# Moving the two layer normalisations of the dense stage from VectorE to ScalarE, with shift and scale worked out on GpSimd

## The reference, cut to what matters

```
out = res + _lin(out, Wf, bf)                          # out: the first attention's result, res: its input
on  = _ln(out, g2, b2)                                 # layer norm with gain and bias
ffn = _lin(relu(_lin(on, Wr1, br1)), Wr2, br2)         # 128 -> 256 -> 128
x   = x + (out + ffn)                                  # called x1 in the kernel
x   = x + _L0_ffn_ref(_layernorm(x), W1, b1, W2, b2)   # 128 -> 512 -> 128, no activation between
```

## Time and profile before

| | us |
|---|---|
| median of 3 runs | 1803.19 |
| lowest and highest run | 1800.59, 1816.49 |
| the profiled execution | 1800.75 |
| its span | 1799.0 |
| the dense stage in it | 822 to 1038 |

### The profile page before, as it was taken

The page is one execution under the profiler, slowest core; times in us unless marked ns, Lnnn a source line. Parts: engine busy times, 40 slices in busy tenths (PEclk is TensorE's granted clock), DMA queues, the critical chain, the costliest instruction groups (busy, mean ns, idle before and its releaser), DMA issues. The chain is left out here.

```text
span 1799.0 us, 45960 instructions
## 1 busy us (share of the span) xinstructions
PE 1516.6 (84%) x13604; PEld 1309.6 (73%) x13668; DVE 1456.8 (81%) x3554; ACT 767.1 (43%) x1731; POOL 866.8 (48%) x1116
## 2 busy tenths in 40 slices
PE   5999999999999999993767648888888888888887
PEld 3999988889889988982655426666666666666665
DVE  5589999999999999974888756778787877777874
ACT  1566656666656665651222213333333333333331
POOL 4356656666666665544565443333333333333331
PEclk8999999999999999996888968999999999999986
DMA  4433222222332222213333133333333333333330
GB/s 137 136 109 90 81 77 79 80 80 86 87 87 87 79 81 77 79 31 94 100 103 87 50 82 93 95 95 95 94 99 93 96 94 96 95 96 97 92 88 17
DMA packets 181693, 158.10 MB, mean 88 GB/s; under 512 B 12529, under 2 KB 163185, under 8 KB 181618
## 3 DMA queue, kind: packets, MB, share of 16 engines
q1 hardware_dynamic: 181618, 157.17, 30.2%
HBM read 113.09 MB, written 44.04 MB: 87 GB/s over the span
## 5 line engine op out<-in xcount | busy, mean ns | idle before, releaser
L587 PE MATMUL a_bank<-a_vp,a_prob 128*128 128x96 f32 x4096 | 635.2, 261 | 0.0
L587 PEld LDWEIGHTS a_bank<-a_vp,a_prob 128*128 128x128 f32 x4096 | 610.6, 192 | 5.6
L481 ACT ACTIVATE a_prob<-a_bank 128x512 f32<-128x512 f32 x512 | 305.9, 598 | 268.2 <-PE a_bank L571 267.3
L675 DVE TENSOR_REDUCE a_nmax<-a_bank 128x2 f32<-128x512 f32 x512 | 345.7, 681 | 49.2 <-PE a_bank L556 41.9
L556 PE MATMUL a_bank<-a_k_st,a_q_st 96*128 96x256 bf16 x1024 | 260.6, 278 | 38.4 <-DVE a_nmax L675 35.4
L571 PE MATMUL a_bank<-a_q_st,a_k_st 120*128 120x256 bf16 x1024 | 281.7, 276 | 3.2 <-POOL a_q_st L344 3.2
L1607 PE MATMUL c_o_bank<-c_vb,c_prob 128*128 128x96 f32 x1024 | 179.4, 301 | 30.1 <-DVE c_ad L1890 29.2
L1765 DVE TENSOR_REDUCE c_nmax<-c_bank 128x4 f32<-128x512 f32 x256 | 166.0, 683 | 38.7 <-PE c_bank L1577 37.1
L344 POOL TENSOR_SCALAR a_q_st<-a_mt 24x2048 bf16<-24x2048 bf16 x64 | 121.4, 1896 | 138.6 <-PE a_bank L571 94.3
L1481 ACT ACTIVATE c_prob<-c_bank 128x256 f32<-128x256 f32 x256 | 98.8, 386 | 186.4 <-PE c_bank L1557 184.8
L1607 PEld LDWEIGHTS c_o_bank<-c_vb,c_prob 128*128 128x128 f32 x1024 | 144.1, 203 | 41.4 <-DVE c_ad L1890 29.1
(11 more groups left out here) (200 smaller groups left out, 3072.4 us busy)
## 6 DMA issues: line engine op xcount, KB each, us to landing
a_q_st<-scratch_a_parts_dram SPq DMA_DIRECT2D x64, 288.0 KB
a_k_st<-scratch_a_parts_dram SPq DMA_DIRECT2D x192, 96.0 KB
c_q_st<-scratch_c_parts_dram SPq DMA_DIRECT2D x64, 288.0 KB
c_k_st<-scratch_c_parts_dram SPq DMA_DIRECT2D x192, 96.0 KB
scratch_a_parts_dram<-a_parts SPq DMA_DIRECT2D x32, 384.0 KB, 2.7
scratch_c_parts_dram<-c_parts SPq DMA_DIRECT2D x32, 384.0 KB, 2.7
a_x<-in_x SPq DMA_DIRECT2D x32, 128.0 KB, 3.2
scratch_y<-a_y SPq DMA_DIRECT2D x32, 128.0 KB, 2.9
```

The costliest lines, as they stand in the source:

```text
L481: act.activation(prob[h % 4][:, :, :].rearrange("p a b -> p (a b)"), t_ps[h % 2][:, :], ACT.Exp).then_inc(exped, 1)
L587: mm = pe.matmul(o_ps[g % 2][:, at:at + VC], prob[h % 4][:, c, t * P:(t + 1) * P], vp[o][:, c, :], start=c == 0, stop=c == NT - 1)
L675: dve.tensor_reduce(nmax[:, t, 2 * g:2 * g + 2], s_ps[t][:, :].rearrange("p (h k) -> p h k", h=2), AX.X, ALU.max, negate=True).then_inc(ma ...
```

## The change

`normed` goes from VectorE's queue to ScalarE's. There it is an activation with the function Identity, `z = rs * r + shift`, with two operands that differ by partition (token). `shift` is `-mean * rs`, which GpSimd's `norm` now works out with two more operations on 128 x 4 numbers, `negm` and `shift`, so that its semaphore counts four steps a unit (NORM = 4). The first normalisation stands between `ao_t` and `on`; the second stands between `on` and the two hidden activations. VectorE gets two waits for the buffers that ScalarE now reads (`x1` and `r`, both two deep), and its waits before the moments are for GpSimd's use of `mv`.

```diff
+        negm, shift = two("negm", [P, C]), two("shift", [P, C])
...
-        N_LOAD, N_LATE = 4, 3
+        N_LOAD, N_LATE, NORM = 4, 3, 4
...
                 pool.tensor_scalar(var[k][:, :], mv[k][:, :, 1], EPS, 1.0, ALU.add, ALU.mult).then_inc(norm_d[k], 1)
-                pool.wait_ge(norm_d[k], 2 * n + 1)
+                pool.tensor_scalar(negm[k][:, :], mv[k][:, :, 0], -1.0, 1.0, ALU.mult, ALU.mult
+                                   ).then_inc(norm_d[k], 1)
+                pool.wait_ge(norm_d[k], NORM * n + 2)
                 pool.tensor_tensor(rs[k][:, :], var[k][:, :], half[:, :], ALU.pow).then_inc(norm_d[k], 1)
+                pool.wait_ge(norm_d[k], NORM * n + 3)
+                pool.tensor_tensor(shift[k][:, :], negm[k][:, :], rs[k][:, :], ALU.mult).then_inc(norm_d[k], 1)
...
+            def normed(k, n, src, dst):
+                act.wait_ge(norm_d[k], NORM * (n + 1))
+                for c in range(C):
+                    act.activation(dst[:, c, :], src[:, c, :], ACT.Identity, scale=rs[k][:, c:c + 1],
+                                   bias=shift[k][:, c:c + 1]).then_inc(z_d[k], 1)
+
...
                 if has(j, u, 1):
+                    if later(j, n, 3):
+                        act.wait_ge(zt_p, n - 2)
+                    normed(0, n - 1, r[1 - i], z[1 - i])
                     act.wait_ge(zt_p, n)
...
+                if has(j, u, 2):
+                    if later(j, n, 4):
+                        act.wait_ge(z1t_p, n - 3)
+                    normed(1, n - 2, x1[i], z1[i])
+                if has(j, u, 1):
                     if later(j, n, 3):
                         act.wait_ge(f_p, n - 2)
...
-            def normed(k, n, src, dst):
-                dve.wait_ge(norm_d[k], 2 * (n + 1))
-                for c in range(C):
-                    dve.tensor_scalar(dst[:, c, :], src[:, c, :], mv[k][:, c, 0:1], rs[k][:, c:c + 1],
-                                      ALU.subtract, ALU.mult).then_inc(z_d[k], 1)
...
                     if later(j, n, 4):
                         dve.wait_ge(xb_d, n - 3)
+                        dve.wait_ge(z_d[1], (n - 3) * C)
...
                     if later(j, n, 3):
-                        dve.wait_ge(z_d[1], (n - 2) * C)
+                        dve.wait_ge(norm_d[1], NORM * (n - 2))
...
                     if later(j, n, 2):
                         dve.wait_ge(xr_d, 2 * (n - 1))
+                        dve.wait_ge(z_d[0], (n - 1) * C)
...
                     if later(j, n, 1):
-                        dve.wait_ge(z_d[0], n * C)
-                if has(j, u, 2):
-                    if later(j, n, 4):
-                        dve.wait_ge(z1t_p, n - 3)
-                    normed(1, n - 2, x1[i], z1[i])
-                if has(j, u, 0):
+                        dve.wait_ge(norm_d[0], NORM * n)
                     moments(0, n, r[i])
```

## The result

| | before | with the change |
|---|---|---|
| median, us | 1809.66 (4 runs, 1800.59 to 1816.49) | 1732.41 (4 runs, 1731.13 to 1735.42) |
| profiled execution | 1800.75 | 1733.57 |
| first stage, to the first load of `dense` | 822.72 | 821.11 |
| dense stage | 215.92 | 175.27 |
| `attention_b`, to the end of the span | 760.36 | 735.42 |

The change took 0.959 of the time before, with a 95% interval of 0.9538 to 0.9641. The forecast was 1763 us with a range of 1752 to 1775, so the sign was right and the time lies 20 us outside the range. The span fell by 67.2 us: 40.65 in the dense stage (forecast 37.7), 24.9 in `attention_b`, whose code is unchanged, and 1.6 in the first stage. The first stage's end lay between 821.4 and 823.1 in all other kernels of this study, none of which alters that stage, so the 1.6 us is mostly spread.

The account below looks back on a forecast made before the run. VectorE's own queue was taken to set the dense stage's 12.21 us step. Twelve steps at 9.6 us save 31.3, plus 3.2 and 3.5, less 0.3: 37.7 us off 1800.75 gives 1763 us, range 1752 to 1775.

Parts of the forecast that it names:

- Removed from VectorE: Dense stage: eight instructions per unit, 5.93 us, and 1.85 us of waits leave VectorE, which no longer bounds anything.
- ScalarE's activation: Added normalisation in the dense stage: 0.49 us per 128x128 activation, 1.66 us per block of four.
- The least and the longest bound: ScalarE's block of four activations: 1.29 us if the second operand is free, 1.96 us without overlap.
- the rival at 1813: GpSimd holds ScalarE's activations as it does VectorE's, 1.26 us each, slower than before; chance 0.02.
- the one at 1811: Rival: ScalarE is the slower engine for normalisation, each block 0.32 us longer, 10 us in all; chance 0.01.
- GpSimd's block: GpSimd's numbers for one normalisation, with negm and shift added: 1.8 us instead of 1.30, bounds 1.7 and 2.1.
- loop A: Dense stage, through GpSimd and ScalarE's second normalisation, hidden activations, second MLP matmul and x1: 9.2 us a unit.
- H: Dense stage loop between second MLP matmuls, through TensorE and ScalarE's first normalisation: 9.2 us a unit.
- TensorE's clock: Granted clock of 0.93 in the dense stage lengthens the loop by 3.8%, 9.55 us; 9.6 taken as the step.
- Filling and draining: Dense stage's ends: 0.3 us lost in filling, 3.2 gained from unit 2 to 3, 3.5 gained at the end.
- the four rivals about the step: Dense steps: 10.4 us (1773, chance 0.13), 8.6 (1750, 0.09), 11.3 or more (1785 up, 0.04), held activations (1813, 0.02).

Follow-up runs that it names:

- e4: The changed kernel with only the first normalisation on ScalarE, the second back on VectorE between r and its moments; 1756.24 us, 0.9714.
- e5: The changed kernel with ScalarE's first normalisation ahead of the copy to ao_t; 1736.26 us, 0.9605.
- e3: The changed kernel with ScalarE's second normalisation behind the two hidden activations, not ahead of them; 1768.79 us, 0.9782.
- e6: The changed kernel with ScalarE's second normalisation behind the hidden activations and TensorE's transpose of z1 behind the second MLP matmul; 1735.72 us, 0.9602.
- e7: The changed kernel with the new orders of e5 and e6 together; 1731.1 us, 0.9568.
- e13: The kernel before with a small GpSimd write in attention_b that puts its last subtraction 0.28 us later; 1735.63 us, 0.9621.
- e12: The changed kernel run once more, unaltered; 1731.16 us, 0.9548.

## Why the prediction was wrong, and where it was right

**What failed** is the first sentence of its reading, "since only the dense stage changes": `attention_b` was carried over at 760 us. It took 735, and in no term of the sum, no rival and no bound was there room for that. I had read a window of that stage for its granted clock, but not asked whether its time is the same whenever it is entered. The spread of the runs shown, 16 us for one and the same program, was a hint that it is not. Of the 29.5 us by which the span's fall exceeded the sum, 24.9 are this stage, 1.6 the first stage, 3.0 the dense stage.

**Removed from VectorE:** as predicted; it is busy 72 us of the dense stage and waits for TensorE.

**ScalarE's activation** was put at 0.49 us and a block at 1.66; measured 482 to 485 ns and 1.65. The least and the longest bound (1.29, 1.96) weren't needed. No activation was held by GpSimd (all 128 took 477 to 496 ns), so the rival at 1813 is out. So is the one at 1811: for this shape VectorE is quicker only where GpSimd rests, and e4 shows the block back at 2.92 us beside it.

**GpSimd's block** was put at 1.8 us plus 0.1 for the hand-over; `var` to ScalarE's block is 1.94. Its work per unit is 8.1 us, not 8.6; GpSimd never fills its step, but through loop A its second block sets the time of most units.

**Loops H and A** were put at 9.2 us each. Where H sets the step it is 8.99, where A does 9.27 to 9.38, and the mean is 9.215: the two loops are right to 0.2 us, and that their mean hits 9.2 this closely is in part luck. e5 shows A by itself near 9.2, and e3 shows what stands behind ScalarE's second block when it comes late. e6 and e7 show what the two sums couldn't: which new loop closes when one is opened.

**TensorE's clock** was to add 0.4 us a unit (9.6), and this term was mis-sized: it added nothing. I took 0.93 from a stage in which TensorE was 85% busy; the six units here ran at 1.00 with 79%. The falls that remain lie mostly in the filling and draining (0.99 from 845 to 980 us), which is why the stage's mean is 0.91. The stage that lent me its 0.93 (1100 to 1300 us) is the very one in which VectorE was held, and e13 ran the same 200 us at 1.00, busy 89%. Twelve steps at 0.4 us are 4.6 us of gain that the forecast left out.

**Filling and draining:** unit 2 to 3 gave 3.5 (forecast 3.2), draining 2.2 (3.5), filling -1.0 (-0.3). Together 4.7 against 6.4.

So 35.9 + 4.7 = 40.6 stands against 31.3 + 6.4 = 37.7, and the four rivals about the step (10.4, 8.6, 11.3 and held activations) did not occur. With 9.2 for the step the forecast would have been 1758, still some 25 us above the profiled execution.

**What stays open:** why the change without a pause falls into the better pattern of `attention_b`. All six kernels with at least one normalisation on ScalarE and no pause (seven profiles, with e12) had 19 held and took 731 to 737 us there; the kernel before and the six with a pause had 31 and took 755 to 772. The starts of the two instructions differ by 0.02 us there, and I found nothing that sets them that finely.

## What to carry to other kernels

Sum the work around each in-order queue as a loop, from one instruction to the same one of the next unit, with a price from a row for each piece: 9.2 for each loop, before I added a clock term, against 9.215 measured as the mean of 8.99 and some 9.3. When a block is moved, write the loops down again, since what leaves one often enters another (e6).

Before calling a stage untouched, look whether two engines that can hold each other start instructions within hundredths of a microsecond there, and whether the same program's runs spread. If so, forecast the stage as several paces; and take the tie away first, for 0.28 us of delay on GpSimd was worth 68 us in the kernel before, more than the change gave in its own stage.

To tell what a change is worth, compare stage by stage: the fall of the medians said 77 us, the stage that was changed 41.

## What the runs showed of the hardware

- A subtraction of VectorE on 64x128 with two SBUF operands takes 0.28 us, or 1.27 when GpSimd's of 1.15 us began 0.02 us earlier. The other way round GpSimd's starts 0.30 us late (e12), or starts 0.08 us late and takes 1.25 to 1.27 us instead of 1.15. In these traces VectorE was held whenever GpSimd's began ahead of it, by 0.01 to 0.11 us, and never when it began behind.
- In the steady part of `attention_b` TensorE's granted clock was 1.00 in each iteration behind a free subtraction and fell to 0.92 or 0.93 in most behind a held one, so that a delay of 1.0 us on one engine cost 2.2 of the stage.
- An activation of 128x128 with two per-partition operands takes 0.48 us on ScalarE, beside a GpSimd busy 87% of the time. The Trainium skill, ScalarE: Activation LUTs, What ACT_TABLE_LOAD costs, gives 186 + 0.833 N ns and about 93 for each such operand, an estimate of 479 ns for this shape; the rows agree.
- TensorE's granted clock was 1.00 over 60 us in which it was busy 79% of the time with no wait above 1.48 us in the stretch. In the kernel before it was 0.86 over a unit in which it was busy 72% and waited 2.95 us for `z1`; the unit ahead of that, with a wait of 2.80 us at its start, ran at 1.00.
